# Token statistics of the first attention on GpSimd, a weight copy three steps ahead, and another order of two evacuations

## What is computed

```python
def _layernorm(x, axis=-1, eps=1e-05):
    m = jnp.mean(x, axis=axis, keepdims=True)
    v = jnp.var(x, axis=axis, keepdims=True)
    return (x - m) / jnp.sqrt(v + eps)
...
# layer 0, attention of 16 heads over a context of 64 rows
    sim = jnp.einsum('bhnd,btd->bhnt', q, k)
    att = jax.nn.softmax(sim, axis=-1)
    y = jnp.einsum('bhnt,btd->bhnd', att, v)
    return y.transpose(0, 2, 1, 3).reshape(b, n, d) @ Wo
...
# layer 1, soft mixture of 16 experts with 64 slots each
    x = _layernorm(x, norm_g, norm_b)
    se = _layernorm(slot_embeds, slot_g, slot_b) * scale
    logits = jnp.einsum('bnd,esd->bnes', x, se)
    dispatch = jax.nn.softmax(logits, axis=1)
    combine = jax.nn.softmax(logits.reshape(x.shape[0], x.shape[1], -1), axis=-1)
    slots = jnp.einsum('bnd,bnes->besd', x, dispatch)
    gate = jax.nn.gelu(jnp.einsum('besd,edf->besf', slots, Wg) + bg[None, :, None, :], approximate=False)
    up = jnp.einsum('besd,edf->besf', slots, Wu) + bu[None, :, None, :]
    eout = jnp.einsum('besf,efo->beso', gate * up, Wd) + bd[None, :, None, :]
...
    return jnp.einsum('bns,bso->bno', combine, eout)
```

## Time and profile before

| | |
|---|---|
| median of 3 runs | 921.48 us (920.25 to 922.68) |
| the profiled execution | 919.0 us, span 917.3 us |
| TensorE | 871.6 us busy (95%) |
| VectorE | 693.3 us (76%) |
| GpSimd | 585.4 us (64%) |
| ScalarE | 533.8 us (58%) |
| chain that ended last, by engine | PE 74%, DVE 13%, ACT 5%, POOL 4%, issue 2%, DMA 1% |

### The profile page before, as it was taken

One profiled execution on the slowest core, in us unless ns is written; L12 is line 12 of the kernel. 1 busy time (PEld: TensorE's weight loads), 2 busy tenths in 40 slices (PEclk: granted clock), 3 DMA queues, 4 the chain that ended last, 5 costly groups with the idle time before them and its releaser, 6 DMA issues.

```text
span 917.3 us, 16060 instructions
## 1 busy us (share of the span) xinstructions
PE 871.6 (95%) x4762; PEld 671.6 (73%) x4762; DVE 693.3 (76%) x1581; ACT 533.8 (58%) x1023; POOL 585.4 (64%) x575
## 2 busy tenths in 40 slices
PE   7898999999898889999999999999999999998997
PEld 5566666666697846888888888888888766775775
DVE  6997776899556788866666666666668768888786
ACT  3555667666662165666666666666666674445465
POOL 6922544688702345877777777777778777888620
PEclk9999999999999989999999999999999998999998
DMA  6000000322100000200000000000002000000001
GB/s 204 1 3 1 2 1 1 98 69 69 29 2 29 2 9 3 71 24 26 26 26 20 23 26 26 26 20 26 23 26 104 1 1 1 1 1 0 1 12 36
DMA packets 27433, 24.46 MB, mean 27 GB/s; under 512 B 3484, under 2 KB 24180, under 8 KB 27252
## 3 DMA queue, kind: packets, MB, share of 16 engines
q1 hardware_dynamic: 27379, 23.80, 8.6%
HBM read 22.74 MB, written 1.05 MB: 26 GB/s over the span
## 4 chain that ended last, share of the span: by engine, by line
PE 74%; DVE 13%; ACT 5%; POOL 4%; issue 2%; DMA 1%; SPq 0%; ACTq 0%; DVEq 0%; POOLq 0%
PE psum L1945 69%; POOL hh L748 2%; ACT hh L876 2%; DVE stats L1400 2%; PE psum L2113 1%; DVE arena L1496 1%; DVE arena L1854 1%; DVE arena L1493 1%; PE psum L2190 1%; ACT arena L937 1%; DVE arena L1505 1%; DVE xn L1419 1%; DVE mv L1403 1%; POOL rstd L659 1%; PE psum L2006 1%
## 5 line engine op out<-in xcount | busy, mean ns | idle before, releaser
L1945 PE MATMUL psum<-xw 128*128 128x512 f32 x1248 | 323.1, 394 | 2.3 <-DVE arena L1747 1.0
L711 POOL TENSOR_TENSOR hh<-arena,hh 128x512 fp32r<-128x512 f32 x176 | 228.2, 1297 | 81.6 <-ACT hh L876 80.2
L1945 PEld LDWEIGHTS psum<-xw 128*128 128x128 f32 x1248 | 232.1, 188 | 55.2 <-issue 3.8
L1754 DVE TENSOR_TENSOR psum<-psum,arena 128x512 f32<-128x512 f32 x176 | 123.0, 699 | 97.7 <-PE psum L1945 91.5
L1119 ACT ACTIVATE arena<-psum 128x512 f32<-128x512 f32 x176 | 105.4, 599 | 120.3 <-PE psum L1945 120.2
L876 ACT ACTIVATE hh<-arena 128x512 fp32r<-128x512 f32 x228 | 142.3, 625 | 38.9 <-DVE arena L1854 35.5
L1945 PE MATMUL psum<-hh,wdn 128*128 128x512 f32 x528 | 148.3, 389 | 0.2 <-POOL hh L711 0.2
L1759 DVE TENSOR_TENSOR arena<-psum,arena 128x512 f32<-128x512 f32 x176 | 121.7, 691 | 7.6 <-DVE psum L1754 1.7
L1945 PEld LDWEIGHTS psum<-hh,wdn 128*128 128x128 f32 x528 | 98.9, 188 | 21.1 <-POOL hh L711 0.5
L1945 PE MATMUL psum<-arena 128*32 128x128 f32 (+6 forms) x992 | 87.1, 305 | 5.4 <-ACT arena L876 3.3
L876 ACT ACTIVATE arena<-psum 128x512 f32<-128x512 f32 (+6 forms) x85 | 57.4, 688 | 47.3 <-PE psum L1945 19.1
(11 more groups left out here) (294 smaller groups left out, 1488.8 us busy)
## 6 DMA issues: line engine op xcount, KB each, us to landing
egu<-in_w SPq DMA_DIRECT2D x44, 128.0 KB, 2.0
egu<-in_egu SPq DMA_DIRECT2D x16, 256.0 KB, 2.6
edn<-in_w SPq DMA_DIRECT2D x44, 64.0 KB, 1.8
edn<-in_edn SPq DMA_DIRECT2D x16, 128.0 KB, 2.1
arena<-in_w SPq DMA_DIRECT2D x1, 1536.0 KB, 6.5
X<-in_x SPq DMA_DIRECT2D x4, 256.0 KB, 5.0
arena<-in_ctxTd SPq DMA_DIRECT2D x2, 512.0 KB, 5.8
arena<-in_conv SPq DMA_DIRECT2D x1, 768.0 KB, 4.4
```

What stands on the lines that cost most here:

```text
L711: pool.tensor_tensor(hh[:, s % 4, 1, :], h1[:, s % 2, :], hh[:, s % 4, 0, :].bitcast(F32), ALU.subtract).then_inc(hh_lo, 1)
L1754: dve.tensor_tensor(bank(2 + k), bank(2 + k), sil[:, k, :], ALU.mult).then_inc(prod_done, 1)
L1945: return pe.matmul(dst, lhsT=lhsT, rhs=rhs, start=start, stop=stop)
```

## The change

Five of the eight normalizations ahead of layers 0 and 1 are computed by GpSimd alone: sums by halving, mean, subtraction, square, sums again, power, product (`token_norm`). VectorE no longer takes their statistics, and `variances` makes the count of `ln_var` fit. GpSimd's list becomes: `keys(1)` to `keys(3)`, `token_norm(0, 2)`, `keys(4)`, `token_norm(0, 3)`, `keys(5)`, `token_norm(1, 0)`, `keys(6)`, `keys(7)`, the slot embeddings, `token_norm(1, 1)`, `token_norm(1, 2)`. The high half of the second expert weights is copied at step q = 29 of the slots stage, ahead of the load of ScalarE's Gelu table, where before it came at the head of the expert loop. `eo_low(6)` comes ahead of the output of expert 15.

```diff
--- before.py
+++ after.py
@@ -452,6 +452,12 @@
             return (L == 0 and g > 0) or (L == 1 and g < NG - 1) or (L == 5 and g < 2) or (L in (4, 6) and g in (1, 3))
 
 
+        STATS_BY_POOL = ((0, 2), (0, 3), (1, 0), (1, 1), (1, 2))
+
+        def variances(L, g):
+
+            return NG * L + g + 1 - sum(own <= (L, g) for own in STATS_BY_POOL)
+
         def applied_by_act(L, g):
 
             return (L in (4, 6) and g == 0) or (L == 5 and g == 2)
@@ -647,7 +653,7 @@
 
             def ln_power(L, g):
                 s = slice(4 * g, 4 * g + 4)
-                pool.wait_ge(ln_var, NG * L + g + 1)
+                pool.wait_ge(ln_var, variances(L, g))
                 if applied_by_act(L, g):
                     pool.tensor_tensor(stats[:, s, 0], wide(zero[:, :], 4), mv[:, s, 0], ALU.subtract)
                 if L == 5:
@@ -661,8 +667,6 @@
                     pool.wait_ge(ln_rstd, NG * L + g + 1)
                     if g >= 1 and not applied_behind(L, g - 1):
                         pool.wait_ge(ln_xn, NG * L + g)
-                    if L == 1:
-                        pool.wait_ge(ln_tp, g + 1)
                     then(pool.tensor_tensor(xn[:, s, :], X[:, s, :], wide(mv[:, s, 0:1], 4, D), ALU.subtract))
                     pool.tensor_tensor(xn[:, s, :], xn[:, s, :], wide(rstd[:, s].unsqueeze(2), 4, D), ALU.mult).then_inc(ln_xn, 1)
 
...
@@ -788,23 +792,49 @@
                         pool.tensor_tensor(kbd[:, b], wide(krep[:, b * C:(b + 1) * C].unsqueeze(1), H0 // 2, C),
                                            wide(rowmask[:, :].unsqueeze(2), H0 // 2, C), ALU.mult).then_inc(kbd_done[1], 1)
 
+                    def sums(half, rows):
+                        then(pool.tensor_tensor(half, rows[:, :, 0:D // 2], rows[:, :, D // 2:D], ALU.add))
+                        n = D // 4
+                        while n:
+                            then(pool.tensor_tensor(half[:, :, 0:n], half[:, :, 0:n], half[:, :, n:2 * n], ALU.add))
+                            n //= 2
+
+                    def slot_sums(rows):
+                        sums(slot_half, rows)
+
+                    def token_norm(L, g):
+                        s, half, sq = slice(4 * g, 4 * g + 4), slot_half[:, 0:4, :], slot_sq[:, 0:4, :]
+                        if L == 0:
+                            pool.wait_ge(x_in[g], 16)
+                        else:
+                            pool.wait_ge(x_done, 4 * g + 4)
+                        sums(half, X[:, s, :])
+                        then(pool.tensor_scalar(mv[:, s, 0], half[:, :, 0], 1.0 / D, None, ALU.mult))
+                        if L == 1:
+                            pool.wait_ge(ln_tp, g + 1)
+                        then(pool.tensor_tensor(xn[:, s, :], X[:, s, :], wide(mv[:, s, 0:1], 4, D), ALU.subtract))
+                        then(pool.tensor_tensor(sq, xn[:, s, :], xn[:, s, :], ALU.mult))
+                        sums(half, sq)
+                        if L == 0:
+                            then(pool.tensor_scalar(veps[:, s], half[:, :, 0], 1.0 / D, EPS, ALU.mult, ALU.add))
+                        else:
+                            then(pool.tensor_scalar(veps[:, s], half[:, :, 0], (1.0 + EPS) / D, EPS * EPS, ALU.mult, ALU.add))
+                        pool.tensor_tensor(rstd[:, s], veps[:, s], neghalf[:, s], ALU.pow).then_inc(ln_rstd, 1)
+                        pool.wait_ge(ln_rstd, NG * L + g + 1)
+                        pool.tensor_tensor(xn[:, s, :], xn[:, s, :], wide(rstd[:, s].unsqueeze(2), 4, D), ALU.mult).then_inc(ln_xn, 1)
+
                     ln_power(0, 0)
                     ln_power(0, 1)
                     pool.wait_ge(krep_done, 1)
-                    keys(1)
-                    ln_power(0, 2)
-                    keys(2)
-                    keys(3)
-                    ln_power(0, 3)
-                    for b in range(4, B):
+                    for b in range(1, 4):
                         keys(b)
-
-                    def slot_sums(rows):
-                        then(pool.tensor_tensor(slot_half, rows[:, :, 0:D // 2], rows[:, :, D // 2:D], ALU.add))
-                        n = D // 4
-                        while n:
-                            then(pool.tensor_tensor(slot_half[:, :, 0:n], slot_half[:, :, 0:n], slot_half[:, :, n:2 * n], ALU.add))
-                            n //= 2
+                    token_norm(0, 2)
+                    keys(4)
+                    token_norm(0, 3)
+                    keys(5)
+                    token_norm(1, 0)
+                    keys(6)
+                    keys(7)
 
                     pool.wait_ge(w_slots, 16 * N_SLOTS)
                     slot_sums(slot_raw)
@@ -815,9 +845,11 @@
                     then(pool.tensor_scalar(srstd[:, 0, :], slot_half[:, :, 0], 1.0 / D, EPS, ALU.mult, ALU.add))
                     then(pool.tensor_tensor(srstd[:, 1, :], srstd[:, 0, :], neghalf[:, 0:ES // P], ALU.pow))
                     pool.tensor_tensor(slot_n, slot_n, wide(srstd[:, 1, :].unsqueeze(2), ES // P, D), ALU.mult).then_inc(se_n, 1)
+                    token_norm(1, 1)
+                    token_norm(1, 2)
                     continue
                 for g in range(NG):
-                    if L != 1 or g < NG - 1:
+                    if L != 1:
                         ln_power(L, g)
                 if L == 1:
 
@@ -984,6 +1016,8 @@
                     ln_evac_group(1, 2 if q == 4 else NG - 1)
                 if q == 4 * B - 4:
                     gate_up0_high(0, 0, 0, 0)
+                if q == 4 * B - 3:
+                    gate_up0_high(1, 0, 0, 1)
                 if q == 4 * B - 2:
                     load_table(ACT.Gelu)
                 if q >= 4 and q % 4 == 1:
@@ -1029,7 +1063,8 @@
                     for f in range(2):
                         n = i * 4 + (2 * k + f)
                         if f == 0:
-                            gate_up0_high(n + 1, i, k, 1)
+                            if later(n, 1):
+                                gate_up0_high(n + 1, i, k, 1)
                         elif k == 0:
                             gate_up0_high(n + 1, i, 1, 0)
                         elif not last:
@@ -1050,9 +1085,9 @@
             expert_pair(E0 // 2 - 1, True)
             load_table(ACT.Exp)
             eo_evac(E0 - 2, 0, E0 // 2 - 1)
+            eo_low(E0 // 2 - 2)
             eo_evac(E0 - 1, 1)
             combine_exp(0)
-            eo_low(E0 // 2 - 2)
             eo_low(E0 // 2 - 1)
             for t in range(1, NT):
                 combine_exp(t)
@@ -1422,7 +1457,7 @@
             def norm_behind(L, t):
 
 
-                if t % 4 == 3 and not (L == 1 and t == NT - 1):
+                if t % 4 == 3 and L != 1:
                     ln_stats(L, t // 4)
                 if t % 4 == 1 and t >= 4 and not applied_behind(L, t // 4 - 1) and not applied_by_act(L, t // 4 - 1):
                     ln_apply(L, t // 4 - 1)
@@ -1494,8 +1529,6 @@
                     if t >= 2:
                         dve.wait_ge(exp_done, t - 1)
                     dve.tensor_tensor(simS[:, t % 2], sim, wide(mx0[:, t % 2, :].unsqueeze(2), H0, C), ALU.subtract).then_inc(sim_used, 1)
-                if t in (0, 2):
-                    ln_stats(0, 2 + t // 2)
                 if t == 5:
                     dve.wait_ge(w_slots, 16 * N_SLOTS)
                     dve.tensor_scalar(slot_gs[:, :], cols[:, COL["slot_g"]:COL["slot_g"] + 2], scal[:, 0:1], None, ALU.mult).then_inc(se_n, 1)
```

More of the change, by code:

```diff
@@ L768, in quantised_norm @@
                     s = slice(4 * g, 4 * g + 4)
-                    pool.wait_ge(ln_var, NG * 7 + g + 1)
+                    pool.wait_ge(ln_var, variances(7, g))
                     then(pool.tensor_scalar(veps[:, s], mv[:, s, 1], EPS, None, ALU.add))
```

## The result

The median of 20 runs after the change is 924.57 us (920.65 to 926.33), that of 20 runs of the kernel before 921.06 us (918.22 to 924.84). The ratio is 1.0033 (95% interval 1.002 to 1.0046), so the change costs about 3.0 us, 1.8 to 4.2 (the plain difference of the two medians is 3.5). The median lies inside the range (918.0 to 926.5), on the slower side of the forecast of +1.2 us, and the ratio just beyond the 0.3% that the prediction calls no change.

What follows compares the result with a forecast made beforehand. VectorE was taken to pace the first attention and TensorE the slots stage behind it. Late group +4.5, weight copy -0.6 and emptied bank -2.7 gave +1.2 us, so 922.7 us, range 918.0 to 926.5.

Steps and rivals of the forecast that it cites:

- rival (b): Behind the slots-stage wait TensorE's clock stays low a second period, perhaps falling at the experts' end too: +3.8 us, 925.3; chance 0.20.
- The gain of the attention: First attention: with five groups of statistics off VectorE, TensorE starts the slot embeddings' transposes 2.9 us earlier; bounds 1.5 and 7.9.
- GpSimd's normalization: One four-row group wholly on GpSimd takes 10.8 us, against 3.2 us today; bounds 10.2 and 11.3.
- rival (a): GpSimd is in time: a group takes 9.4 us or less, so TensorE never waits for (1, 2): 915.3 us; chance 0.15.
- Its dates: GpSimd's list in the first attention: early entries in time, (1, 1) at 80.2 just in time, (1, 2) late at 91.0.
- The late group: TensorE waits for (1, 2) ahead of the slots stage: +4.5 us with the clock's fall; bounds +0.5 and +7.2.
- The way from GpSimd's first product to T2: Slots stage: from GpSimd's first product at 91.0 to dispatch transpose 2 at about 95.9, +3.0 us at full clock.
- The low clock: After some 6 us idle before the slots stage, TensorE runs at 1.2 GHz for 3.4 us, costing 1.6 us more.
- The weight copy: Start of the experts: copying the second expert weights' high half early removes TensorE's 0.66 us wait: -0.6; bounds 0 and -0.7.
- The emptied bank: End of the experts: bank 6 freed early lets the combining products start sooner at full clock: -2.7 us; bounds -1.8 and -2.8.
- The sum: Whole kernel: slots-stage cost less the two small edits' gains, +4.5 - 0.6 - 2.7 = +1.2 us.

Runs made afterwards that it cites:

- the repetition: The kernel after, unaltered, run again on the chip of a kernel with 24 unread filler products: 923.64 us, ratio 1.0029.
- the statistics alone: The change without the early weight copy and the early eo_low, so only the five normalizations on GpSimd: 928.06 us, ratio 1.0084.
- four groups: The changed kernel with the statistics of (0, 2) back on VectorE, the other four on GpSimd: 922.92 us, ratio 1.0023.
- copy alone: The kernel before with only the weight copy three steps ahead: 920.79 us, ratio 0.9995.
- small edits: The kernel before with the weight copy three steps ahead and eo_low before the last eo_evac, statistics unmoved: 919.20 us, ratio 0.9988.
- the delay: The kernel before with 12 unread units on TensorE ahead of the transpose of (1, 2): 924.32 us, ratio 1.003.
- the last outputs alone: The kernel before with only eo_low(6) ahead of the output of expert 15: 919.69 us, ratio 0.9985.
- three groups: The changed kernel with (1, 0) and (1, 1) back on VectorE; GpSimd keeps (0, 2), (0, 3), (1, 2): 917.12 us, ratio 0.9968.

## Why the prediction was right, and where it missed

The forecast was +1.2 us, measured were +3.0. The range holds it by its width on the slower side; by the number alone rival (b), +3.8 us, came nearer than the forecast.

**The gain of the attention**: predicted 2.9 us, measured 3.06. The turns in which TensorE's order holds VectorE back are there. VectorE's timeline of after, at turns 7 and 11, waits for the scores:

```profile
40.05 1.23 DVE L1528 TENSOR_REDUCE arena<-psum 128x16 f32<-128x1024 f32 x1 [0.76 <-PE psum L1978]
...
56.95 1.22 DVE L1528 TENSOR_REDUCE arena<-psum 128x16 f32<-128x1024 f32 x1 [0.89 <-PE psum L1978]
```

**GpSimd's normalization**: predicted 10.8 us for a group, measured 10.83 (69.55 to 80.38) and 10.82. The line through three sizes holds at four rows; rival (a) needed 9.4. The prediction has today's GpSimd without a pause from 13.84 on; it paused 1.15 us at 14.9 and 0.92 at 21.3, for the statistics of (0, 2) and (0, 3), which the dates of the new list don't need. **Its dates**: (1, 1) at 80.2 and (1, 2) at 91.0, measured 80.4 and 91.25. Where the prediction had (1, 1) just in time, TensorE waited 1.03 us for it; that wait lies ahead of the longer one and adds nothing.

**The late group**: this is the term of the sum that was mis-sized. It was put at +4.5 (its parts, 3.0 and 1.6, add up to 4.6) and measured +5.57. The way from GpSimd's first product to T2 was right, 4.9 us predicted and 5.05 at full clock, but it began at 91.20, not 91.0, so this part is +3.4. The low clock was put at 3.4 us long from the release on, for 1.6 us. In the profile of after it was 6.8 us long, began at 89, while TensorE was still idle, and had 4.7 us of work in it, for 7.26 - 5.05 = 2.2 us; in other profiles of the same wait it cost 1.3 (the repetition), 2.1 (the statistics alone) and 2.5 (four groups). The length was taken from a single stretch, behind 2.30 us of idle time; in all four profiles of the 6 us wait it was 6.8. The trace of before had longer rows already, which rival (b) names; this is the length, though not the end of experts, that rival (b) assumed.

**The weight copy**: predicted 0.6, measured 0.40. With the wait for GpSimd gone, TensorE waits 0.31 us at the next group, for the smallest logits of VectorE (L1602). **The emptied bank**: predicted 2.7, measured 2.63 and, alone, 2.82.

**The sum** at R: +1.2 predicted, +2.5 measured, of which the low clock is 0.6, the late date and the longer way 0.4 and the copy 0.2. The +2.5 hangs on the one profile of before, which has no low clock ahead of 249. The three profiles with before's lists up to the slots stage that had two early stretches were 1.9 to 2.3 us later there (copy alone, small edits, the delay); the last outputs alone had none and was 0.1 later. Where GpSimd sets the date, T2 was at 98.2 to 98.8 with an early stretch or without. Against an execution of before with early stretches the cost at R would be 0.2 to 0.6 us only. **The whole**: +3.0, 1.8 to 4.2, agrees with +2.5.

What the sum doesn't have is the low clock elsewhere. Up to the end of its span the profile of before has 29 us of it and that of after 38, most of it at places where neither kernel differs from the other. One row of the same work, after first:

```profile
776.00:778.00 2.00, 2.00 (x6) 1.57 (x5) 0.95 (x3) 0.63 (x1) 1.67 (x2) 0.50 0.00 0
```

```profile
776.00:778.00 2.00, 2.00 (x11) 1.65 (x10) 1.92 (x4) 0.87 (x2) 1.73 (x3) 1.00 0.00 0
```

Behind R the profile of after took 665.95 us with 31 us of low clock, that of before 663.07 with 26. But the repetition of after took 662.69, with 22: the same kernel, 3.3 us less, without the stretches at 293 to 298 and 867 to 871. So the stretches fall differently from one execution of a kernel to the next, some of them (16 to 20, 79 to 85) ahead of every edit, and a difference of 3 us between two single profiles behind R says nothing of the change. Besides, the profile of before is a good one, 2 us under the median of its runs.

That a change of the kernel moves the stretches as well is likely, and not shown. The gains came out smaller in the whole than in their place (-3.0 and -1.1 for the small edits, -5.1 and -2.9 for three groups), and the mean granted clock of the runs points the same way: three groups have 0.9804 against 0.9823, though their kernel has no stretch at 249. No experiment separates this from chance. So the profiles account for about +2.5 of the +3.0; the remaining 0.5 is within the interval of the ratio.

## What to carry to other kernels

Work that goes to an idle engine has to be entered into that engine's list date by date: it is not the sum of the idle time that must suffice, but the time between each input and each use. The kernel with one early group less lost as much as the full change; the kernel that kept the early two and the last and gave back the two between won. And a wait that idles TensorE for several microseconds can cost more than the date that it moves; here 1.3 to 2.5 us of low clock came on top of 3.4. Single profiles should be compared from a common event on (here GpSimd's first product), not by their times from the start.

## What the runs showed of the hardware

The same idle time doesn't always bring the low clock. TensorE idled 1.90 us ahead of the transposes at 79.54 in the kernel before and stayed at 1.00, and the same 1.90 us ahead of 80.58 in the small edits, where the clock fell 0.7 us later, for 3.4 us. Nor does it always take idle time. In the profile of after TensorE shows no wait after 747.2, and its clock fell at 758.2, for 6.8 us:

```profile
757.00:758.00 1.00, 1.00 (x11) 1.00 (x11) 0.65 (x8) 0.70 (x2) 0.98 (x1) 1.00 0.00 0
...
759.00:760.00 1.00, 1.00 (x6) 1.00 (x6) 0.32 (x5) 0.10 (x1) 1.00 (x2) 0.50 0.00 0
```

The stretches were near 3.4, 6.8 and 10.2 us long. Of the 3.4 us long ones, that at 16 to 20 cost the path 1.0 us and that at 81 to 85 1.3 (small edits).

VectorE's small instruction is stretched beside GpSimd also where it works on four columns. With three groups on GpSimd, VectorE's step behind the statistics took 0.97 and 0.74 us, where the same one took 0.17 before. Both engines' timelines:

```profile
39.89 3.05 POOL L794 TENSOR_TENSOR arena<-arena,rowmask 128x512 f32<-128x512 f32 x3
40.98 0.97 DVE L1448 TENSOR_SCALAR veps<-mv 128x4 f32<-128x4 f32 x1
...
57.23 1.90 POOL L849 TENSOR_TENSOR arena<-arena 128x1024 f32<-128x1024 f32 x1
58.41 0.74 DVE L1448 TENSOR_SCALAR veps<-mv 128x4 f32<-128x4 f32 x1
```

The second ends at 59.15 with the GpSimd instruction at 59.13, the first at 41.95, where the second of three GpSimd instructions of 1.02 us ends. The large reduces beside them were not longer than in the earlier trace rows (1.22 and 1.23 us).
